# An adaLN transformer block: four changed orders, and three modulation rows multiplied in hi and lo parts during the first swiglu pass

## The reference

```python
mod = (_silu(L0_c) @ L0_wmod).reshape(L0_c.shape[0], 6, 1, -1)
sa, ca, ga, sb, cb, gb = (mod[:, i] for i in range(6))
ga, gb = (2 * (g >= 0) - 1) * jnp.maximum(jnp.abs(g), 0.25)      # for each of the two
h = _layernorm(x) * (1 + ca) + sa
x = x + ga * attn(h)       # qkv, running sums of exp(k) and exp(k)*v, sigmoid(q), swiglu 512 -> 2048 -> 512
h = _layernorm(x) * (1 + cb) + sb
x = x + gb * ffn(h)        # a shared gelu FFN, and 8 experts of which each token takes 2
```

## Time and profile before

| | us |
|---|---|
| median of 3 runs | 1939.67 (1938.92 to 1943.29) |
| the profiled execution | 1936.98 |
| its span | 1935.2 |
| TensorE busy in the span | 1893.0 (98%) |
| VectorE busy | 1279.0 (66%) |
| ScalarE busy | 650.1 (34%) |
| GpSimd busy | 284.7 (15%) |

### The profile page before, as it was taken

One profiled execution on the slowest core, in us unless ns is written; L12 is line 12 of the kernel. 1 busy time (PEld: TensorE's weight loads), 2 busy tenths in 40 slices (PEclk: granted clock), 3 DMA queues, 4 the chain that ended last, 5 costly groups with the idle time before them and its releaser, 6 DMA issues.

```text
span 1935.2 us, 26114 instructions
## 1 busy us (share of the span) xinstructions
PE 1893.0 (98%) x8882; PEld 1536.5 (79%) x8882; DVE 1279.0 (66%) x2639; ACT 650.1 (34%) x1309; POOL 284.7 (15%) x251
## 2 busy tenths in 40 slices
PE   7999999999999999999999999999998999999998
PEld 4688888878888888888888888888886777788886
DVE  6789999875545554556356456557556565599997
ACT  4677776621111111123112212222222332344443
POOL 0000000000000000000001011011020230388885
PEclk9999999999999999999999999999998999999999
DMA  5313112321110211025012422312344776588886
GB/s 189 135 49 104 54 50 66 131 78 64 66 56 10 77 66 44 22 90 182 23 65 82 116 68 82 138 68 82 116 133 183 249 227 216 180 156 154 153 153 97
DMA packets 88990, 206.74 MB, mean 107 GB/s; under 512 B 9781, under 2 KB 26454, under 8 KB 81772
## 3 DMA queue, kind: packets, MB, share of 16 engines
q1 hardware_dynamic: 65292, 144.55, 21.8%
q0 software_dynamic: 23568, 60.51, 14.7%
HBM read 126.95 MB, written 80.51 MB: 107 GB/s over the span
## 4 chain that ended last, share of the span: by engine, by line
PE 81%; POOL 8%; issue 4%; DVE 4%; DMA 3%; ACT 1%; POOLq 0%; SPq 0%; DVEq 0%; ACTq 0%
PE bank L697 13%; PE bank L699 13%; PE bank L698 13%; PE bank L702 12%; PE bank L704 11%; PE bank L703 11%; POOL out L661 5%; POOL rows_t L651 3%; DMA xs<-columns 2%; PE bank L716 1%; PE bank L731 1%; PE bank L761 1%; PE bank L772 1%; PE bank L765 1%; PE bank L869 1%
## 5 line engine op out<-in xcount | busy, mean ns | idle before, releaser
L697 PE MATMUL bank<-x_hi,w_blk 128*128 128x512 f32 x1024 | 403.2, 394 | 3.4 <-DVE s_t L1622 2.3
L699 PE MATMUL bank<-x_hi,w_blk 128*128 128x512 f32 x1024 | 399.5, 390 | 0.0
L698 PE MATMUL bank<-x_lo,w_blk 128*128 128x512 f32 x1024 | 399.2, 390 | 0.0
L1622 DVE TENSOR_TENSOR s_t<-act_t,bank 128x512 f32<-128x512 f32 x128 | 87.9, 687 | 272.7 <-PE bank L699 259.1
L1239 ACT ACTIVATE s_hi<-s_t 128x512 fp32r<-128x512 f32 x128 | 80.9, 632 | 436.2 <-DVE s_t L1622 417.3
L697 PEld LDWEIGHTS bank<-x_hi,w_blk 128*128 128x128 f32 x1024 | 192.7, 188 | 43.1 <-DVE w_blk L1418 2.7
L699 PEld LDWEIGHTS bank<-x_hi,w_blk 128*128 128x128 f32 x1024 | 192.6, 188 | 40.8
L698 PEld LDWEIGHTS bank<-x_lo,w_blk 128*128 128x128 f32 x1024 | 192.7, 188 | 38.9
L702 PE MATMUL bank<-w_blk,s_hi 128*128 128x512 f32 x512 | 199.9, 390 | 0.0
L704 PE MATMUL bank<-w_blk,s_lo 128*128 128x512 f32 x512 | 199.4, 390 | 0.0
L703 PE MATMUL bank<-w_blk,s_hi 128*128 128x512 f32 x512 | 199.3, 389 | 0.0
(11 more groups left out here) (272 smaller groups left out, 3445.1 us busy)
## 6 DMA issues: line engine op xcount, KB each, us to landing
x_t<-y_scratch SPq DMA_DIRECT2D x16, 1024.0 KB, 5.1
residual<-r_t SPq DMA_DIRECT2D x16, 1024.0 KB, 4.3
r_t<-residual SPq DMA_DIRECT2D x16, 1024.0 KB
columns<-hT SPq DMA_DIRECT2D x16, 1024.0 KB, 6.3
xs<-columns SPq DMA_DIRECT2D x16, 1024.0 KB, 8.7
raw<-w_swi POOLq DMA_DIRECT2D x16, 768.0 KB, 4.4
y_scratch<-y_t SPq DMA_DIRECT2D x32, 256.0 KB, 2.7
r_t<-x_tok SPq DMA_DIRECT2D x8, 1024.0 KB
```

Of the source, the lines that this page charges most:

```text
L697: nc.tensor.matmul(dst, w[:, 0, col:col + P], rhs_hi, start=start, stop=False)
L698: nc.tensor.matmul(dst, w[:, 0, col:col + P], rhs_lo, start=False, stop=False)
L699: return nc.tensor.matmul(dst, w[:, 1, col:col + P], rhs_hi, start=False, stop=stop)
L1622: nc.vector.tensor_tensor(s_t[:, s % 2, :], act_t[:, s % 2, :], bank[4 + (2 * s + 1) % 3][:, :], ALU.mult).then_inc(f.s_ok, 1)
```

## The change

It has these parts.

1. Rows sb, cb and gb are no longer made in the first stage. Each is made once in pass b, in tiles 1, 2 and 3. SyncE loads the 1 MB of wmod into `m_raw` behind the x load of the tile before. ScalarE rounds it in four pieces (`row_hi`, at s = 0 to 3), VectorE takes the rest (`row_lo`). At s = 5 TensorE does eight matmuls (`late_row`): the stationary operand `c_2` has 34 columns, hi of c in columns 0-1 and lo of c in 32-33. ScalarE copies rows 32-33 (`row_rest`, s = 6), VectorE adds them (`row_sum`, s = 7), SyncE stores the row. `c_parts` makes `c_2` once, in tile 0 at s = 6.
2. `take_shift(1)` moves on ScalarE from group 1 to group 0, behind the two exponentials.
3. In pass b tile 0, `rows_for_b(0)` moves from s = 2 to s = 1, statistics and residual from s = 2 and 3 to 6 to s = 3 and 4 to 7; only the gain row of the sequence at hand is fixed, so that of sequence 1 is fixed in tile 4.
4. In pass s, `load_half(3)` goes ahead of `second_norm_out(LAST)`, and `load_half(2t + 2)` goes to the front of iteration t.
5. In the slots `gb_row` has two buffers and is made at the end of the iteration before (`slot_gain`), ahead of the register load of an expert index.

```diff
@@ sync, first stage
-                    sp.wait_ge(mod_mm, 4)
-                    load_wmod(3)
-                    load_wmod(4)
-                if 2 <= g < 6:
+                if g == 2:
                     store_mod(g)
-                if g == 3:
-                    sp.wait_ge(mod_st, 16 * (2 * NB_SEQ + 2))
-                    load_wmod(5)
@@ sync, pass b, tile t
+                if 1 <= t <= 3:
+                    sp.wait_ge(mr.row_ok, t)
+                    sp.dma_start(mod_dram[MOD_ORDER[t + 2]], m_row[:, :]).then_inc(mod_st, 16)
+                if t < 3:
+                    sp.wait_ge(mr.lo_ok, NC * t)
+                    sp.wait_ge(y_st, 16 * NG)
+                    sp.dma_start(m_raw[:, :], wmod[MOD_ORDER[t + 3]]).then_inc(mr.raw_in, 16)
                 sp.wait_ge(ffn["b"].ev_ok, NSUB * (t + 1))
@@ sync, pass s
             gates_in(0)
+            load_half(3)
             second_norm_out(LAST)
             for t in range(NT):
+                if 0 < t < LAST:
+                    load_half(2 * t + 2)
                 if t == 1:
                     hT_out(LAST)
...
                 if t + 1 < NT:
                     gates_in(t + 1)
-                if t < LAST:
-                    if t > 0:
-                        load_half(2 * t + 2)
+                if 0 < t < LAST:
                     load_half(2 * t + 3)
@@ tensor, first stage
-                if 3 <= g < 7:
-                    pe.wait_ge(mod_row, g - 2)
+                if g == 3:
+                    pe.wait_ge(mod_row, 1)
...
-                if 1 <= g < 5:
+                if g == 1:
                     pe.wait_ge(a.lo_ok, g + 2)
                     modulate(bank_h[0:NB_SEQ, :], g + 1, lambda m: c_t[:, m * NB_SEQ:(m + 1) * NB_SEQ])
@@ tensor, pass b
+            def late_row(t):
+                pe.wait_ge(mr.lo_ok, NC * t)
...
+                for m in range(NC):
+                    ins = nc.tensor.matmul(b_x[0:32 + NB_SEQ, :], c_2[:, m, :], ch(m_hi, m), start=(m == 0), stop=(m == NC - 1))
+                    for k in range(NC if m == 0 else 0):
+                        nc.tensor.matmul(b_x[0:NB_SEQ, :], c_2[:, k, 0:NB_SEQ], ch(m_lo, k), start=False, stop=False)
+                ins.then_inc(mr.mm, 1)
...
+                        if p == "b" and 1 <= t <= 3 and s == 5:
+                            late_row(t)
                         if s >= 2:
                             down(p, t, s - 2, w_blk[:, place(s - 2), :, :], 2 * QKV_W, NB)
@@ scalar, first stage
-                if g == 1:
-                    take_shift(1)
...
                 if g == 0:
+                    take_shift(1)
                     seed_spread(1)
@@ scalar, pass b
+            def row_hi(t, m):
+                act.wait_ge(mr.raw_in, 16 * t)
+                act.wait_ge(mr.mm, t - 1)
+                nc.scalar.activation(ch(m_hi, m), ch(m_raw, m), ACT.Copy).then_inc(mr.hi_ok, 1)
@@ vector, pass b
             def rows_for_b(q):
                 dve.wait_ge(bc_in, 16 * (4 if q == 0 else 6))
-                if q == 0:
-                    fix_gain(ga_t[0], tmp[0])
-                    fix_gain(ga_t[1], tmp[1])
+                fix_gain(ga_t[q], tmp[0])
...
+                            if t == 0 and s == 1:
+                                rows_for_b(0)
                             if t == 0 and s == 2:
                                 quotient(NG - 1)
-                                rows_for_b(0)
...
-                            if s == 2:
+                            first = 3 if t == 0 else 2
+                            if s == first:
                                 dve.wait_ge(r_in, 16 * (t + 1))
                                 token_stats()
+                            if 1 <= t <= 3 and s < NC:
+                                row_lo(t, s)
@@ vector, slots
+            def slot_gain(j):
+                if j >= 2:
+                    dve.wait_ge(rt.o_ok, j - 1)
+                if j < 2:
+                    dve.wait_ge(ffn["s"].ev_ok, NSUB * LAST + 3 + j)
+                nc.vector.scalar_tensor_tensor(out=gb_row[j % 2][:, :], in0=gbd_t[:, :], scalar=late_t[:, j:j + 1],
+                                               in1=gbs_t[0][:, :], op0=ALU.mult, op1=ALU.add).then_inc(rt.gr_ok, 1)
```

More of the change, by code:

```diff
@@ L111, in build @@
         hrow = at("hrow", 16, [P, NSUB, D])
+        m_raw = at("m_raw", 0, [P, CHW])
+        m_hi = at("m_hi", 8, [P, CHW], F32R)
+        m_lo = at("m_lo", 16, [P, CHW], F32R)
+        c_2 = at("c_2", 24, [P, NC, 32 + NB_SEQ], F32R)
+        m_rest, m_row = at("m_rest", 26, [NB_SEQ, D]), at("m_row", 28, [NB_SEQ, D])
         cb1, sbb, gbb, gb_t = [at(n, 24 + 2 * i, [P, D]) for i, n in enumerate(("cb1", "sbb", "gbb", "gb_t"))]
@@ L268, in build @@
         gw_ok = sem("gw_ok")
+        c2_ok = sem("c2_ok")
+        mr = sems("late_rows", "raw_in hi_ok lo_ok mm rest_ok row_ok")
         xs_in = [sem(f"xs_in{k}") for k in range(3)]
@@ L899, in gates_to_rows @@
                 ins.then_inc(n2.gt_tr, 1)
+            def late_row(t):
+                pe.wait_ge(mr.lo_ok, NC * t)
+                if t == 1:
+                    pe.wait_ge(c2_ok, 1)
+                else:
+                    pe.wait_ge(mr.row_ok, t - 1)
+                for m in range(NC):
[3 more added lines that the diff above has]
+                ins.then_inc(mr.mm, 1)
             pe.wait_ge(a.kv_ok, NG - 1)
@@ L1286, in _ @@
                             piece_hi(i)
+                        if p == "b" and 1 <= t <= 3 and s < NC:
+                            row_hi(t, s)
+                        if p == "b" and 1 <= t <= 3 and s == 6:
+                            row_rest(t)
                         if p == "c" and t >= 1:
@@ L1870, in gate_weights, with c_parts, row_lo, row_sum @@
                                         ALU.add).then_inc(gw_ok, 1)
+            def c_parts():
+                dve.wait_ge(a.cum, 3 * NG)
+                from_ = c_t[:, :].rearrange("p (m q) -> p m q", m=NC)
+                nc.vector.memset(c_2[:, :, NB_SEQ:32].bitcast(F32), 0.0)
+                then(nc.vector.tensor_copy(c_2[:, :, 0:NB_SEQ], from_))
+                nc.vector.tensor_tensor(c_2[:, :, 32:32 + NB_SEQ], from_, c_2[:, :, 0:NB_SEQ].bitcast(F32),
+                                        ALU.subtract).then_inc(c2_ok, 1)
+            def row_lo(t, m):
+                dve.wait_ge(mr.hi_ok, NC * (t - 1) + m + 1)
+                nc.vector.tensor_tensor(ch(m_lo, m), ch(m_raw, m), ch(m_hi, m).bitcast(F32), ALU.subtract).then_inc(mr.lo_ok, 1)
+            def row_sum(t):
+                dve.wait_ge(mr.rest_ok, t)
+                if t > 1:
+                    dve.wait_ge(mod_st, 16 * (2 * NB_SEQ + t))
+                nc.vector.tensor_tensor(m_row[:, :], b_x[0:NB_SEQ, :], m_rest[:, :], ALU.add).then_inc(mr.row_ok, 1)
             def hT_lo(u, g):
@@ L1886, in _ @@
                                 sum_kv(NG - 1)
+                            if t == 0 and s == 1:
+                                rows_for_b(0)
                             if t == 0 and s == 2:
                                 quotient(NG - 1)
-                                rows_for_b(0)
                             if t == T_SEQ and s == 2:
                                 rows_for_b(1)
-                            if s == 2:
+                            first = 3 if t == 0 else 2
+                            if s == first:
                                 dve.wait_ge(r_in, 16 * (t + 1))
                                 token_stats()
-                            if 3 <= s < 3 + NSUB:
-                                first_residual(t, s - 3)
+                            if first < s <= first + NSUB:
+                                first_residual(t, s - first - 1)
+                            if 1 <= t <= 3 and s < NC:
+                                row_lo(t, s)
+                            if 1 <= t <= 3 and s == 7:
+                                row_sum(t)
+                            if t == 0 and s == 6:
+                                c_parts()
                             if t == 0 and s == 7:
```

21 lines of the change are left out of this document (12 added, 9 removed).

## The result

| | before | changed |
|---|---|---|
| median, us | 1939.67 (1935.32 to 1943.29, 5 runs) | 1925.98 (1925.26 to 1926.89, 5 runs) |
| profiled execution, its span | 1936.98, 1935.2 | 1925.73, 1923.9 |
| TensorE / VectorE busy | 1893.0 / 1279.0 | 1886.9 / 1284.6 |

The ratio is 0.9927 [0.9917, 0.9937], 13.7 us less. The forecast was 1925.5. The same kernel timed again later, in a larger set (`e9_changed_again`), was 15.1 us faster than before, 0.992 [0.9907, 0.9934]. Its single executions, over both sets, lie between 1919.3 and 1926.9, and the experiments name one cause of that spread.

What follows compares the result with a forecast made beforehand. TensorE's list was taken to bound the kernel nearly everywhere; -10.4 + 5.4 - 3.2 - 2.3 - 1.6 - 2.0 - 0.1 = -14.2 us took the median from 1939.67 to 1925.5, range 1916 to 1930.

Steps and rivals of the forecast that it cites:

- Part 1a: First stage: three modulation rows leave TensorE's list at 3.53 us each, less a 0.2 us wait; -10.4 us.
- Part 1b: Pass b: the same rows add 24 matmuls at 0.227 us, everything else hidden at zero cost; +5.4 us.
- rival 4: Pass b tiles 1 to 3: m_raw lands late, stalling TensorE and dropping the clock; slower, 1949 at 8 us stalls; chance 0.02.
- rival 2: First stage: VectorE limits groups 2 to 5, giving 4 us back, 1929.5 us; chance 0.09.
- Part 2: First stage: moving take_shift removes TensorE's wait before the first sums, with no clock won back; -3.2 us.
- Part 3: Pass b tile 0: the new order removes TensorE's 2.3 us wait on block 3's product; -2.3 us.
- Part 4, the first xs wait: Pass s: the 7.74 us wait goes, a 6.1 us wait for hT_lo 2 follows with low clock; -1.6 us.
- rival 1: Pass s: the first xs wait goes with its clock and nothing follows; 1916.9 us; chance 0.13.
- Part 4, the later xs waits: Pass s: the even half goes earlier, freeing DMA engines sooner; -2.0 us, bounds -3.0 and +3.0.
- rival 5: Pass s: the xs loads collide anew, +3 us instead of -2, 1930.5 us; chance 0.10.
- Part 5: Slots: the register load moves between gain and output, VectorE not being what TensorE waits for; -0.1 us.
- rival 3: Slots: VectorE held them after all, 5 us more gained, 1920.5 us; chance 0.04.

Runs made afterwards that it cites:

- e9: The changed kernel itself, unedited, timed again in a later set: 1924.70 us (1919.31 to 1926.27).
- e8: Changed kernel with take_shift(1) put back in group 1: 1930.88 us, one execution.
- e2: Changed kernel with the earlier order of pass b tile 0 (rows_for_b(0) with both fix_gain, and statistics, at s = 2): 1930.26 us, one execution.
- e3: Changed kernel with load_half(2t + 2) for t of 1 to 6 put back beside load_half(2t + 3): 1927.18 us, ratio 0.9917.
- e5: Changed kernel with VectorE's block (1, 0) and hT_lo 2 ahead of evacuate_s(0), and hT_out(LAST) behind load_half(5): 1920.27 us, ratio 0.9891.
- e4: Changed kernel with GpSimd's last eight list writes put behind the landing of half 9: 1926.16 us, ratio 0.9916.
- e6: e5 with load_gain(1), a 256 KB load, moved from iteration 3 to iteration 1: 1917.24 us, ratio 0.9875.
- e12: e6 with the next tile's even half issued right behind the out store, and the last list writes behind half 9's landing: 1914.31 us, ratio 0.9871.
- e7: Changed kernel without GpSimd's last eight list writes (tile 7's routed tokens left out of the lists): span 1938.7 us.

## Why the prediction was right, point by point

**Part 1a**, -10.4 forecast, -10.9 measured between two landmarks (three rows of 3.77 us are 11.3). The working held. The small error is the 0.2 us per row that stand around the eight records and not in them.

**Part 1b**, +5.4 forecast, +5.6 measured. A stationary operand of 34 columns, or of 2, cost what the row with 128 did: 0.23 us for 512 moving columns. All that was put at zero was zero; rival 4 did not come about, and neither did rival 2, since the groups came to 10.01 us without a wait for VectorE.

**Part 2**, -3.2 forecast, -3.1 measured (-3.4 counted from the stage's own start, which came 0.3 us later in the trace of after). It was right for that pair of traces. "No clock is won back" holds there, but e8 shows that the clock can fall behind this wait, so over many executions the part may be worth somewhat more.

**Part 3**, -2.3 forecast, -4.1 between the traces, of which -2.55 is the order (e2). The stretch at 406 to 410 was not looked at ahead: its clock of 0.56 would have shown the rest.

**Part 4, the first xs wait**, -1.6 forecast, -1.1 measured. The place of the new wait, its releaser and the fall of the clock came as worked out, and rival 1 fell with them. Two sizes were off, against each other. The first was the r_t load: from its issue to VectorE's start it took 5.9 us before with an xs load issued behind it, and 5.8 after with none behind it (5.7 to its landing). The row chosen, 4.8 us for x_t, is of another load of 1 MB. The wait was 7.2 instead of 6.1 us, 1.0 us lost. The second was the price of the clock: matmuls start 0.43 us apart only from 1484.96 to 1488.61, which costs 1.8 us where the forecast had 2.5 from the kernel before, 0.7 us won. By the rule of the Trainium skill cited ahead ("DMA: Bandwidth & Descriptors", "Queues, rings and completion order") r_t would come no sooner and this part be -0.5; the trace agrees that the load behind it did not hold r_t up.

**Part 4, the later xs waits**, -2.0 forecast. The execution of 1919.31 has that number (-1.9 over tiles 3 and 4, by their distances 27.3 and 26.0 before, 25.4 and 26.0 in e9). The one of 1925.73 has rival 5: -1.9 in tile 3, +5.0 in tile 4, together +3.1, the upper bound named. A load of 1 MB that ends 2.5 us later decides between them, and the clock doubles it. The mechanism named for this term, the even half that goes earlier, is not borne out: e3 puts the even halves back and keeps the 1.9 us of tile 3. What brought them stays open.

**Part 5**, -0.1 forecast, -0.7 in this pair and -1.2 in e9's trace against before. In all twelve traces with this order and the whole lists the stretch takes 248.7 to 249.5 us, against 250.0 in the one trace of before. It was not isolated and stays open; rival 3's -5 is excluded.

The sum of -14.2 stands against -11.3 in the first pair of spans, -17.7 in e9's, and -13.7 and -15.1 in the medians. The terms that missed cancel in part: 1.8 too little in part 3 (0.25 of it the order, the rest the clock), 0.5 in part 1a and 0.6 in part 5, against 0.5 too much in the first xs part and up to 5.1 in the later one. That the median of 1925.98 lies within 0.5 us of the forecast 1925.5 is therefore luck in part. The profiled execution of before lay 2.7 us under its median and that of the changed kernel 0.25 under its own, so 2.4 of the 13.7 us between the medians belong to no part that the pair of traces shows. What was not luck is parts 1 and 2 to half a microsecond each and the place of the new wait. The chances as stated add up to 0.90; no case was named for the rest.

## What to carry to other kernels

Where one engine's list fills the span, work taken out and put in can be priced from the distances of starts, to half a microsecond here. Work on waits is different: the 7.7 us wait went first to VectorE's order (7.2), then to transfer volume (7.5), and it was gone when order and stores had both been moved (e5). With the loads moved too the kernel is 11 us faster than by the change alone. Before one moves a load, list who waits next and who shares the DMA engines with it; a load that depends on nothing goes ahead of those that wait for something. `load_half(3)` is such a load, and its wait went. When one load is slow now and then, compare several executions before an edit is given the credit: e3, e4 and e6 are not told apart from the kernels that they edit.

## What the runs showed of the hardware that was not expected

- Behind a wait of 7.0 to 7.7 us in the midst of the work TensorE's clock was at 0.50 in all ten traces that have one. In pass s waits for xs of 2.3 to 4.7 us did the same in nine traces (readings of 0.50 to 0.66 behind them), and one of 1.3 us did not (1.00, e9). Earlier in the kernel it was not the same each time: after 2.3 us it fell to 0.56 in one kernel and stayed at 1.00 in another with the same wait; after 3.2 us it stayed once and fell once. It also read 0.57 to 0.69 at 18 to 22 us in three executions (e3, e5, e8), which put the next modulation row 1.7 to 2.4 us later than in the changed kernel's trace. In the one pair of executions that was compared stretch by stretch, a later half 9 and the clock behind it make 5.1 of 6.4 us.
- The load of half 9 (1 MB) took 15.3 to 18.7 us with the eight list writes beside it (eleven traces), 9.6 us without them in e12, and at most 12.9 and 13.2 in e7 and e4. The writes are small: in e4 the engines moved 0 to 1 GB/s from 1562 to 1565, with the writes alone. Beside them the engines are full at 69 to 145 GB/s, where they move over 400 elsewhere.
- Two loads of 1 MB differed: x_t took 4.8 us at the median, r_t 5.7 in the changed kernel with no other large transfer beside it. The trace has 144 packets for the first of these x_t loads and 597 for r_t with the small gate load; that the packets are the reason was not tested.
